# A decoder layer in one program: the fourth exponential ahead of two copies in narrow tiles, and two buffers for head groups' outputs

## What is computed

```
q = (x @ Wq).reshape(B, T, H, Dh)      # k, v alike; B = 4, T = 512, H = 16, Dh = 32
scores = einsum('bthd,bshd->bhts', q, k)
scores = scores * tril(ones(T, T))     # masked scores are 0, not minus infinity
attn = softmax(scores / T ** 0.5, axis=-1)
out = einsum('bhts,bshd->bthd', attn, v).reshape(B, T, H * Dh)
return out @ Wo
```

## Time and profile before

| | us |
|---|---|
| median of 3 runs (lowest, highest) | 1473.67 (1473.34, 1474.0) |
| the profiled execution's own time | 1473.66 |
| its span | 1471.9 |
| PE busy | 1421.3 (97%) |
| DVE busy | 990.5 (67%) |
| ACT busy | 711.1 (48%) |
| POOL busy | 385.6 (26%) |

### The profile page before, as it was taken

The page is one execution under the profiler, slowest core; times in us unless marked ns, Lnnn a source line. Parts: engine busy times, 40 slices in busy tenths (PEclk is TensorE's granted clock), DMA queues, the critical chain, the costliest instruction groups (busy, mean ns, idle before and its releaser), DMA issues.

```text
span 1471.9 us, 26844 instructions
## 1 busy us (share of the span) xinstructions
PE 1421.3 (97%) x8896; PEld 719.8 (49%) x8896; DVE 990.5 (67%) x2125; ACT 711.1 (48%) x1648; POOL 385.6 (26%) x703
## 2 busy tenths in 40 slices
PE   6999998999999999999999999999999999999999
PEld 4465456556645654344444444444444444444444
DVE  7786688678658867896666566666656755666533
ACT  5795279239616945344353353353353443533532
POOL 0053225304373536521221211112111211212100
PEclk9999999999999999999999999999999999999999
DMA  7554622352455511010100001001001001000011
GB/s 250 133 170 125 165 77 82 112 161 70 142 161 162 191 64 46 17 33 17 33 17 16 23 13 31 17 17 35 17 17 33 17 17 33 17 17 1 0 58 57
DMA packets 77309, 98.01 MB, mean 67 GB/s; under 512 B 8048, under 2 KB 60784, under 8 KB 76784
## 3 DMA queue, kind: packets, MB, share of 16 engines
q1 hardware_dynamic: 77168, 96.23, 21.2%
HBM read 68.94 MB, written 27.26 MB: 65 GB/s over the span
## 4 chain that ended last, share of the span: by engine, by line
PE 84%; issue 5%; DVE 4%; ACT 4%; POOL 2%; DMA 0%; ACTq 0%; POOLq 0%; DVEq 0%; SPq 0%
PE bank L887 25%; PE bank L888 24%; PE bank L889 24%; PE bank L951 2%; PE bank L972 2%; ACT prob L1268 2%; PE bank L900 1%; PE bank L940 1%; PE bank L1012 1%; PE bank L1027 1%; POOL nmx L766 1%; PE bank L981 1%; PE bank L1022 1%; DVE xt L1591 1%; PE bank L1033 1%
## 5 line engine op out<-in xcount | busy, mean ns | idle before, releaser
L887 PE MATMUL bank<-xs,G 128*128 128x512 f16 x896 | 339.8, 379 | 1.7 <-DVE c L1736 0.9
L889 PE MATMUL bank<-xs,G 128*128 128x512 f16 x896 | 339.6, 379 | 0.0
L888 PE MATMUL bank<-xs,G 128*128 128x512 f16 x896 | 339.6, 379 | 0.0
L1736 DVE TENSOR_TENSOR c<-bank,c 128x512 f32<-128x512 f32 x128 | 88.1, 689 | 192.7 <-PE bank L889 192.7
L1354 ACT COPY c<-bank 128x512 f32<-128x512 f32 x192 | 111.2, 579 | 220.3 <-PE bank L889 215.5
L887 PE MATMUL bank<-Wd,hid 128*128 128x512 f16 x512 | 194.1, 379 | 2.8 <-DVE X L1790 2.8
L888 PE MATMUL bank<-Wd,hid 128*128 128x512 f16 x512 | 194.0, 379 | 0.0
L889 PE MATMUL bank<-Wd,hid 128*128 128x512 f16 x512 | 194.0, 379 | 0.0
L751 POOL TENSOR_TENSOR c<-c,m 128x512 f32<-128x512 f32 x64 | 82.4, 1288 | 388.4 <-ACT c L1354 388.4
L1790 DVE SCALAR_TENSOR_TENSOR X<-bank,col,X 128x512 f32<-128x512 f32 x128 | 95.4, 750 | 101.5 <-PE bank L889 101.3
L1606 DVE CUSTOM_DVE_ANT_0 bank<-bank,mask,col 128x128 f32<-128x128 f32 (+3 forms) x256 | 139.1, 548 | 20.4 <-issue 14.9
(11 more groups left out here) (193 smaller groups left out, 2402.9 us busy)
## 6 DMA issues: line engine op xcount, KB each, us to landing
stack<-qk_dram SPq DMA_DIRECT2D x128, 128.0 KB, 3.3
sc_in<-scale_t SPq DMA_DIRECT2D x30, 384.0 KB
qk_dram<-qk SPq DMA_DIRECT2D x32, 256.0 KB, 2.8
packed_t<-pk_t SPq DMA_DIRECT2D x32, 192.0 KB, 1.9
pk_in<-packed_t SPq DMA_DIRECT2D x30, 192.0 KB
X<-in_x_dram SPq DMA_DIRECT2D x4, 1024.0 KB, 5.8
pk_in<-L_ffn_gate_W_packed_dram SPq DMA_DIRECT2D x16, 256.0 KB, 2.7
pk_in<-n_L_ffn_up_W_packed_dram SPq DMA_DIRECT2D x16, 256.0 KB, 3.1
```

The lines of the kernel that those rows point to most:

```text
L887: pe.matmul(o, lhs(0), rhs(0), start=first, stop=False, skip_group_check=onto)
L888: pe.matmul(o, lhs(0), rhs(1), start=False, stop=False, skip_group_check=onto)
L889: return pe.matmul(o, lhs(1), rhs(0), start=False, stop=stop, skip_group_check=onto)
L1736: nc.vector.tensor_tensor(dst[:], bank[at][:], dst[:], ALU.add).then_inc(comb, 1)
```

## The change

It has two parts.

1. On ACT, in units with i = 0 or 1, heads 0 and 1 of the unit are copied out of the turning banks after the fourth exponential and `e_zero`; before, the copy of head 0 stood between the third and the fourth exponential.
2. There are two `o_sum` buffers, for even and odd head groups. The second is the upper half of `c_in`. POOL's `out_tail` of group r - 2 now stands in the first unit of group r (i = 0, slot 3), for r = 2 and 3, and that of group 2 behind the last unit; before, `out_tail` of r - 1 stood in the third unit of group r. `divide` waits for the tail of two groups before instead of the group before. Since `c_in` is in use until the attention ends, SP loads the next context after the last group's tail and not in the third quarter of the attention.

```diff
-        o_sum = sb("o_sum", [P, T], F32)
+        o_sums = [sb("o_sum", [P, T], F32)[:], c_in[:, 2:4].rearrange("p t c -> p (t c)")]
...
-                    if not last and r == 2:
-                        load_ctx(n + 1)
...
                 if not last:
+                    sp.wait_ge(o_lo, (n + 1) * HG)
+                    load_ctx(n + 1)
                     stack_heads(n + 1, range(2 * HG))
...
-                        if j == 3 and i == 2 and r > 0:
-                            out_tail(n, r - 1)
+                        if j == 3 and i == 0 and r > 1:
+                            out_tail(n, r - 2)
+                out_tail(n, HG - 2)
...
                         if j == 3 and u % TT < TT - 1:
                             exp_zero(n, u)
-                        if j >= 2:
+                        if j == 3 and u % TT < 2:
+                            turned(n, u, 0)
+                            turned(n, u, 1)
+                        elif j >= 2 and u % TT >= 2:
                             turned(n, u, j - 2)
...
-                if i == 0 and hg > 0:
-                    dve.wait_ge(o_hi, n * HG + hg)
-                    dve.wait_ge(o_lo, n * HG + hg)
+                if i == 0 and hg == 1:
+                    dve.wait_ge(ct_full, n * 2 + 2)
+                if i == 0 and hg > 1:
+                    dve.wait_ge(o_lo, n * HG + hg - 1)
...
-                nc.vector.scalar_tensor_tensor(o_sum[:, P * i:P * i + P], ...
+                nc.vector.scalar_tensor_tensor(o_sums[hg % 2][:, P * i:P * i + P], ...
```

More of the change, by code:

```diff
@@ L783, in out_head @@
                     pool.wait_ge(xf_stored, n * 16 + 16)
-                nc.gpsimd.tensor_copy(o_t[:, 0, hg, :], o_sum[:]).then_inc(o_hi, 1)
+                nc.gpsimd.tensor_copy(o_t[:, 0, hg, :], o_sums[hg % 2]).then_inc(o_hi, 1)
             def out_tail(n, hg):
                 pool.wait_ge(o_hi, n * HG + hg + 1)
-                nc.gpsimd.tensor_tensor(o_t[:, 1, hg, :], o_sum[:], o_t[:, 0, hg, :], ALU.subtract).then_inc(o_lo, 1)
+                nc.gpsimd.tensor_tensor(o_t[:, 1, hg, :], o_sums[hg % 2], o_t[:, 0, hg, :], ALU.subtract).then_inc(o_lo, 1)
             def sum_part(h, step):
@@ L1293, in out_head @@
                 act.wait_ge(o_done, n * UNITS + 4 * hg + 4)
-                nc.scalar.copy(o_t[:, 0, hg, :], o_sum[:]).then_inc(o_hi, 1)
+                nc.scalar.copy(o_t[:, 0, hg, :], o_sums[hg % 2]).then_inc(o_hi, 1)
             def repacked(n, r):
@@ L1638, in divide @@
                 hg, i = u // TT, u % TT
-                if i == 0 and hg > 0:
-                    dve.wait_ge(o_hi, n * HG + hg)
-                    dve.wait_ge(o_lo, n * HG + hg)
+                if i == 0 and hg == 1:
+                    dve.wait_ge(ct_full, n * 2 + 2)
+                if i == 0 and hg > 1:
+                    dve.wait_ge(o_lo, n * HG + hg - 1)
                 dve.wait_ge(rden_out, n * UNITS + u + 1)
                 dve.wait_ge(av_done, n * UNITS + u + 1)
-                nc.vector.scalar_tensor_tensor(o_sum[:, P * i:P * i + P], bank[6][:, P * (u % 2):P * (u % 2) + P], QS, r_den[:, u % 2, :],
+                nc.vector.scalar_tensor_tensor(o_sums[hg % 2][:, P * i:P * i + P], bank[6][:, P * (u % 2):P * (u % 2) + P], QS, r_den[:, u % 2, :],
                                                ALU.mult, ALU.mult).then_inc(o_done, 1)
@@ L1648, in out_tail @@
                 dve.wait_ge(o_hi, n * HG + hg + 1)
-                nc.vector.tensor_tensor(o_t[:, 1, hg, :], o_sum[:], o_t[:, 0, hg, :], ALU.subtract).then_inc(o_lo, 1)
+                nc.vector.tensor_tensor(o_t[:, 1, hg, :], o_sums[hg % 2], o_t[:, 0, hg, :], ALU.subtract).then_inc(o_lo, 1)
             def repacked(n, r):
```

## The result

| | before | changed |
|---|---|---|
| median, us (4 runs each, side by side) | 1473.51 (1472.92 to 1474.0) | 1464.96 (1464.15 to 1465.19) |
| ratio, 95% interval | 1 | 0.994 (0.9928 to 0.9952) |
| span of the profiled execution, us | 1471.9 | 1463.2 |
| PE / DVE / ACT / POOL busy, us | 1421.3 / 990.5 / 711.1 / 385.6 | 1418.3 / 992.6 / 711.9 / 386.7 |

The change takes 8.55 us off; 8.0 were forecast. In what follows, (i, j) is again head j of tile i, and E the end of the row sum of exponential (3, 3).

The account below looks back on a forecast made before the run. ACT was taken as the fullest engine, losing time only where it waits. 2 x 0.47 + 0.37 + 0.70 = 2.01 us a batch, 8.0 for four, gives 1465.7 us, range 1462.5 to 1470.8.

Parts of the forecast that it names:

- Part 1 at i = 1: At i = 1, the fourth exponential fills ACT's wait before copy (1, 0); exponential (2, 0) starts 0.37 us earlier.
- Part 1 at i = 0: At i = 0, the fourth exponential fills ACT's wait before copy (0, 0); packed weights' cast starts 0.21 us earlier.
- The `shift` is a limit at i = 1: Exponential (2, 0) waits for its `shift`, done at E + 6.82, so gain is 0.37 us instead of 0.52.
- ACT becomes the only bound: Rival: `shift` (2, 0) is no limit; 1.8 us more saved, 1463.9 us; chance 0.64 shared with the forecast.
- Part 2, `divide`: At i = 3: `divide`'s 0.84 us wait goes, exponentials (3, 0) to (3, 3) take 2.99 us, not 3.24.
- The give-back: (3, 3)'s row sum ends 0.94 us after its start instead of 0.79, so of 0.25 us only 0.09 arrives.
- The batch's end: From group 3's exponential (3, 0) to PE's next-batch transposes: 0.70 us less, 4.8 instead of 5.5.
- The groups: Steady group from E to E takes 14.28 us instead of 14.75: 0.47 less, two such spans a batch.
- Part 2 alone: Rival: only part 2 counts, i = 2 comes no earlier; 3.5 us less, 1470.1 us; chance 0.18.
- The tail's cover: POOL's tail at i = 0 ends at E + 2.70, next maximum about E + 3.0: 0.3 us cover, cost 0.
- Given back between attentions: Rival between attentions: gain lost to stores behind the context or FFN-start weight load; about 1472 us; chance 0.11.
- slower: Rival at i = 0 and 1: copies late for PE in 28 narrow units; 1483.1 us; chance 0.07.

Follow-up runs that it names:

- e4: Changed kernel with the new order on ACT only at i = 1, the order of before at i = 0; 1468.16 us.
- e9: Changed kernel, PE's packed-weight transposes and ACT's cast moved from i = 0 to i = 1, DVE's cast to i = 2; 1465.58 us.
- e12: e9 with ACT's order of before in the narrow tiles (part 1 undone); 1468.14 us.
- e5: Changed kernel with DVE's cast of packed weights behind the second row maximum of i = 1 instead of ahead of it; 1464.17 us.
- e7: Changed kernel with both the moves of e5 and e6; 1464.39 us.
- e2: Changed kernel with ACT's order of before, so part 2 alone (two buffers, tail's new place, context later); 1469.40 us.
- e1: Kernel before with only the order on ACT changed (part 1 alone), one `o_sum` buffer, tail in the third unit; 1470.61 us.
- e8: Changed kernel with one more operation of the tail's size on POOL just ahead of the tail at i = 0; 1464.97 us.
- e6: Changed kernel with PE's first scores of i = 2 ahead of the values of i = 3; 1464.78 us.
- e3: Changed kernel with both buffers kept, but POOL's tail of the group just finished put back to i = 2; 1465.68 us.

## Why the prediction was right, step by step

- **Part 1 at i = 1: right.** Forecast E + 3.61, 4.58, 5.19 and 5.65 for the four exponentials; measured 3.61 (228.07), 4.57, 5.18, 5.64. Copies E + 6.20, measured 6.19. `shift` (2, 0) done at E + 6.82, measured 231.11 + 0.19 = E + 6.84; exponential (2, 0) at E + 6.85, measured 6.88.
- **Part 1 at i = 0: right, tested.** The cast comes earlier because the exponential no longer waits with the copy; e4 without this step loses 2.8 us by the trace, and e9 and e12 show that it works through the cast alone: with the cast moved away, the order at i = 0 has no effect.
- **The `shift` is a limit at i = 1: right in time, incomplete in cause.** "ACT becomes the only bound" would have saved 1.8 us more. The prediction named one limit, the maxima behind DVE's cast. e5 to e7 take that one and the next away and gain nothing; PE's chain behind ACT's cast is just as long. The forecast came out because all of them hang on the same cast.
- **Part 2, `divide`: right, tested.** 2.99 us from (3, 0) to (3, 3) as forecast; e2 alone shortens i = 3 from 4.38 to 4.14 us with the old order of ACT, and e1 keeps the 0.85 of idle time.
- **The give-back (0.94 instead of 0.79 us of result delay): right in kind.** In the changed kernel it is 224.46 - 223.59 = 0.87. In e2, with part 2 alone, it is 0.91, and i = 0 takes 3.59 us instead of 3.47: there all 0.12 come back.
- **The batch's end: mis-sized.** 0.80 us measured, 0.70 forecast, in four places: 0.4 us of the 0.55 by which the median beat the forecast. The 0.70 borrowed from group 0 that DVE's copy starts 1.60 us behind exponential (3, 0). In the changed kernel it still does so in group 0 (1.59), but 1.50 in group 3 (1.56 in e2); why is open.
- **The groups: slightly mis-sized, two errors that partly cancel.** i = 2 takes 3.54 instead of 3.50 us; the smaller give-back (0.07) and an i = 1 that is 0.03 shorter more than make up for it. Two steady groups save 1.04 where 0.94 was forecast, and group 1's beginning and group 3's first part 0.33 where it was 0.37.
- **Part 2 alone: mis-sized.** Forecast 3.5 us, e2 measured 4.8 by the medians and 4.0 by the trace. With part 1 alone (2.5 forecast for it in the experiments) it falls short of the whole: the parts help each other, which the prediction didn't speak of as such, though its sum was made with both.
- **The tail's cover: mis-sized, without effect.** Forecast 0.3 us, measured 0.77 of idle time, and e8 puts 1.16 more there for nothing. The estimate took the maximum of (1, 0) behind PE's scores at E + 3.0 as the deadline; the `shift` ran at 227.49 = E + 3.03, so the deadline was right, but the tail began at E + 1.10, not at E + 1.54. The last `shift` of i = 0 starts at E + 0.95 where it started at E + 1.35, in e2 at E + 0.97 and in e1 at E + 1.34: it is part 2, the missing wait of `divide`, that brings DVE's maxima forward, which the prediction had not counted. The tail takes 1.16 to 1.17 us at either place. The contention that the Trainium skill warns of (GPSIMD Engine Reference, "Key points") is not tested by that: as the tail runs in its new place, from 225.56 to 226.73, DVE has only the copy out of a PSUM bank that starts at 225.27, and then nothing, so no VectorE instruction with two SBUF inputs ran beside it.
- **The rest moves as a block: right.** 0.01 us between two attentions, with the context's load behind the last tail and ahead of the q and k stores. "Given back between attentions" and "slower" did not happen: PE has no new wait for a `prob_t` copy in i = 0 or 1 (the one at i = 0 of group 0 grew from 0.17 to 0.27 us, and that tile takes 4.47 us as before), and the exponentials of i = 2 show no wait for `nmx`.

Of the 0.56 us a batch that the two parts give more together than apart, the tail's collision in e1 accounts for 3 x 0.13, and the shorter result delay for 0.05 in each of the two steady groups and again at the batch's end (4.70 us against e2's 4.75). What stays open is why this delay is 0.91 us in e2 and 0.86 in the changed kernel, which differ only in the order on ACT at i = 0 and 1.

## What to carry to other kernels

When an engine waits in front of an instruction while work for it is ready behind, moving that work ahead costs nothing and is worth the wait that it fills, but count it at the next engine's limit: here 0.54 + 0.38 us of waits gave 0.40 us a group. Look for the one instruction on which several chains hang (here the cast that frees a bank): what comes earlier with it is gained on all of them, while none of the three kernels that went after a wait which the trace names gained anything. A single buffer between a producer and two readers costs as much as its slow reader stands in the way at the worst place, and that may be a place that comes once a batch (0.80 us here) rather than the one that comes every group (0.25).

## What the runs showed of the hardware that was not expected

**The opening runs at either clock level.** Columns of the two windows: length, PE, PEld, DVE, ACT, POOL, granted clock, DMA share, GB/s; the first is of before, the second of the changed kernel.

```profile
24.00:28.00 4.00, 4.00 (x12) 1.49 (x11) 3.66 (x6) 4.00 (x8) 0.00 (x0) 0.57 0.62 207
```

```profile
24.00:28.00 4.00, 4.00 (x21) 1.44 (x20) 3.93 (x6) 4.00 (x8) 0.00 (x0) 1.00 0.66 219
```

The granted clock was 0.57, 0.58, 0.62 and 0.59 of full speed in the profiles of before, e1, e4 and e6, that is the 1.2 GHz level for most of this stretch, and 1.00 in the other ten. The first exponential of i = 1 came at 71.8 to 72.2 us in the four and at 70.6 to 71.3 in the ten. PE had been idle for about 2.4 us ahead of its first 128x512 product in before, and in e2, e5, e8, e9 and e12 as well, which had the full clock. So this doesn't go with that idle time. Nor does it go with the kernel. The mean granted clock of the whole execution is 0.999 in the four profiles and 1.000 in the ten, and in their other executions kernels show both: the changed kernel run again took 1463.68 to 1464.12 us in three executions at 1.000 and 1465.08 and 1465.24 in two at 0.999; the kernel before, beside it, 1472.92 on average in eight and 1473.84 in seven. That 0.999 means the same 4 us there too is inferred from the profiles, not seen. It puts about 1 us of chance into any single comparison, more than several of the differences asked for here.

**One result of ACT comes 0.79 to 0.96 us after its start, depending on what went before.** From the start of exponential (3, 3) to the end of its row sum it is 0.94 to 0.96 us in group 0 of every kernel. In the later groups it is 0.79 to 0.80 before and in e1, 0.82 to 0.83 in e3, 0.85 to 0.87 in the changed kernel and most others, 0.90 to 0.91 in e6 and e7 and 0.91 to 0.92 in e2. Within a kernel it repeats to 0.02 us. It was longer where `divide` no longer held ACT up at i = 3; what sets it between 0.82 and 0.92 wasn't tested. The difference is not free: what waits for the row sum comes later by it (i = 0 in e2).
